# Targets read from SBUF, their PSUM bank given to layer 3 and the scores, in a DIN attention kernel on one core

## The reference

```
tgt = concat([target, pos]) @ proj_w + proj_b
din = concat([tgt, seq, tgt - seq, tgt * seq])
h = sigmoid(din @ w1 + b1)
h = sigmoid(h @ w2 + b2)
score = (h @ w3 + b3)[..., 0]
score = where(mask == 0, -1e9, score)
out = einsum('bs,bsd->bd', softmax(score), seq)
```

## Time and profile before

| What | Value |
|---|---|
| Median of 3 runs | 293.26 us |
| Profiled execution, time | 293.81 us |
| Its span | 292.0 us |
| Granted TensorE clock, mean over the span | 0.972 of full |
| TensorE busy | 250.3 us (86%) |
| VectorE busy | 235.7 us (81%) |
| GpSimd busy | 193.7 us (66%), all but 2 us of it after 66.3 us |
| ScalarE busy | 154.7 us (53%) |
| DMA queue of SyncE | 82.3% of 16 engines' span |

### The profile page before, as it was taken

How to read it: one execution, slowest core, us unless ns; L and a number is a source line. 1 busy time by engine, 2 the same in 40 slices (tenths; PEclk the granted TensorE clock), 3 DMA queues, 4 the chain that set the end, 5 groups by cost and what they waited for, 6 DMA issues and landing times.

```text
span 292.0 us, 5476 instructions
## 1 busy us (share of the span) xinstructions
PE 250.3 (86%) x2084; PEld 77.9 (27%) x2084; DVE 235.7 (81%) x331; ACT 154.7 (53%) x257; POOL 193.7 (66%) x125
## 2 busy tenths in 40 slices
PE   4659999999999999999999999999999999998100
PEld 2213323222322232323223323322233223222000
DVE  3598999689687886896887868968968799549696
ACT  2003467665666476556755674666566647656100
POOL 2000000009979979979799799797997997987970
PEclk9999999999999999999999999999999999999855
DMA  6989999999799999999999999899898860431200
GB/s 117 167 125 175 162 176 261 214 165 309 126 202 284 179 329 145 161 326 162 270 214 176 323 171 272 201 154 319 130 178 304 133 270 0 136 153 29 114 0 18
DMA packets 216749, 53.68 MB, mean 184 GB/s; under 512 B 209556, under 2 KB 210068, under 8 KB 216724
## 3 DMA queue, kind: packets, MB, share of 16 engines
q1 hardware_dynamic: 211640, 52.70, 82.3%
q10 hardware_dynamic: 5084, 0.64, 1.4%
HBM read 53.20 MB, written 0.13 MB: 183 GB/s over the span
## 4 chain that ended last, share of the span: by engine, by line
DVE 47%; PE 33%; issue 11%; POOL 3%; SPq 2%; DMA 1%; ACT 1%; DVEq 0%; ACTq 0%; POOLq 0%
DVE X L550 15%; PE pA L389 12%; DVE X L541 11%; DVE HidA L676 10%; PE pB L399 8%; PE pA L435 7%; DVE mix_v L637 3%; DVE HidB L683 2%; PE pA L445 2%; PE pL L415 2%; POOL mix L519 2%; POOL mix L508 1%; DVE pB L644 1%; PE pL L422 1%; DMA proj_b<-in_L_rec_proj_b 1%
## 5 line engine op out<-in xcount | busy, mean ns | idle before, releaser
L519 POOL TENSOR_TENSOR mix<-mix 128x260 f32<-128x260 f32 (+5 forms) x51 | 96.9, 1900 | 5.2 <-POOL acc L512 0.5
L277 ACT ACTIVATE HidA<-HidA,VA 128x512 f32<-128x512 f32 x100 | 66.8, 719 | 52.7 <-DVE HidA L676 52.7
L286 ACT ACTIVATE G<-pL,bias 128x512 f32<-128x512 f32 x100 | 60.5, 688 | 47.0 <-PE pL L422 47.0
L508 POOL TENSOR_TENSOR mix<-seq_sb,E 128x4096 f32<-128x4096 f32 (+3 forms) x13 | 77.2, 5941 | 0.4 <-POOL acc L523 0.3
L550 DVE SCALAR_TENSOR_TENSOR X<-pT,P_pair,X 128x512 f32<-128x512 f32 x100 | 69.8, 739 | 0.2
L676 DVE TENSOR_TENSOR HidA<-pA,UA 128x1024 f32<-128x1024 f32 x50 | 59.8, 1196 | 4.6 <-PE pA L389 4.2
L541 DVE STREAM_TRANSPOSE X<-squares 128x1024 f32<-128x1024 f32 x50 | 61.7, 1235 | 0.0
L389 PE MATMUL pA<-X,w_seq 64*64 64x512 f32 x400 | 55.0, 621 | 4.3 <-DVE HidA L676 3.7
L506 POOL MEMSET masked<- 128x64 f32 x11 | 1.7, 152 | 82.5 <-ACT E L319 82.5
L389 PE MATMUL pA<-X,w_sb 64*64 64x512 f32 x400 | 53.7, 608 | 0.0
L399 PE MATMUL pB<-X,wB 128*32 128x512 f32 x400 | 47.8, 596 | 0.0
(11 more groups left out here) (96 smaller groups left out, 106.1 us busy)
## 6 DMA issues: line engine op xcount, KB each, us to landing
squares<-in_L_rec_sequence_emb SPq DMA_DIRECT2D x98, 256.0 KB, 4.7
seq_sb<-in_L_rec_sequence_emb SPq DMA_DIRECT2D x12, 2048.0 KB, 9.9
seq_sb<-in_L_rec_sequence_emb SPq DMA_DIRECT2D x1, 1024.0 KB, 5.1
squares<-in_L_rec_sequence_emb ACTq DMA_DIRECT2D x2, 256.0 KB, 6.1
mask_i<-in_r_mask SPq DMA_DIRECT2D x1, 400.0 KB, 5.5
tgt_sb<-in_L_rec_target_emb SPq DMA_DIRECT2D x1, 128.0 KB, 2.2
out_dram<-result SPq DMA_DIRECT2D x1, 128.0 KB, 2.0
w_sb<-in_L_rec_w ACTq DMA_DIRECT2D x1, 80.0 KB, 3.8
```

Of the source, the lines that this page charges most:

```text
L277: last = nc.scalar.activation(h, h, ACT.Tanh, scale=0.5, bias=VA[:, 4 * u + i:4 * u + i + 1])
L286: nc.scalar.activation(G[p % NG][:, :], pL2[p % 4][:, :], ACT.Tanh, scale=0.5, bias=bias2[:, 0:1])\
L508: nc.gpsimd.tensor_tensor(mix[:, 0:k, 0:n, 0:D], seq_sb[c % RING][:, 0:k, 0:n, :], e[:, 0:k, 1:n + 1].unsqueeze(3).to_broadcast([P, k, n, ...
L519: nc.gpsimd.tensor_tensor(mix[:, 0:k, 0:n, :], mix[:, 0:k, 0:n, :], mix[:, 0:k, n:2 * n, :], ALU.add)\
```

## The change

`products` reads the targets from `T2` in SBUF in place of `pT` in PSUM, so all three operands of L550 are in SBUF. The bank `pT` is free for layer 3's scores and, after ScalarE has copied these out, for the transposed scores and the softmax step (`bank3`, `bank_st`); the last block uses two banks of `pL2`. `pA` is left to layer 1, so the waits on `s_za` in `layer3` and `transpose_scores` go, and so do two waits ahead of `layer1_first`. The copy to `rows` is made one iteration later, in the iteration of the transposes, ahead of layer 2's four Tanh. The transposes of the scores go ahead of `layer2_last`. On VectorE the second `transpose_quad` of an iteration goes ahead of the first pair's product, and the second pair's product goes behind the second `targets_first`. `shared_bank` becomes the two halves of `pA` and `pB`.

```
-    L2_LAG, L3_LAG, ST_LAG = 1, 2, 3
+    L2_LAG, L3_LAG, ROWS_LAG, ST_LAG = 1, 2, 3, 3
...
-        pL3, pST = pA[:, 0:512], pA[:, 512:1024]
+        def bank3(c):
+            return pT if c < NBLK - 1 else pL2[0]
+
+        def bank_st(c):
+            return pT if c < NBLK - 1 else pL2[1]
...
-        shared_bank = {SHARED: pT, SHARED + 1: pB, SHARED + 2: pL2[0]}
+        shared_bank = {SHARED: pA[:, 0:512], SHARED + 1: pA[:, 512:1024], SHARED + 2: pB[:, :]}
...
-                if 0 <= g < NGRP:
-                    for j in range(4):
-                        second_layer(4 * g + j)
-                c = block_of_last_group(n - L3_LAG)
+                c = block_of_last_group(n - ROWS_LAG)
                 if c is not None:
                     act.wait_ge(s_l3, c + 1)
                     if c > 0:
                         act.wait_ge(s_st, c)
+                    nc.scalar.activation(rows[:, :].rearrange("p (r k) -> p r k", k=SQ),
+                                         bank3(c)[:, :].rearrange("p (k r) -> p r k", r=TILE), ACT.Identity,
+                                         bias=bias3[:, 0:1]).then_inc(s_rows, 1)
+                if 0 <= g < NGRP:
+                    for j in range(4):
+                        second_layer(4 * g + j)
...
-            def layer3(c, quads):
-                pe.wait_ge(s_za, quads)
-                if c > 0:
-                    pe.wait_ge(s_rows, c)
+            def layer3(c):
+                if 0 < c < NBLK - 1:
+                    pe.wait_ge(s_soft, SOFT * c)
...
-            def transpose_scores(c, quads):
-                pe.wait_ge(s_za, quads)
-                if c > 0:
-                    pe.wait_ge(s_soft, SOFT * c)
+            def transpose_scores(c):
                 pe.wait_ge(s_rows, c + 1)
...
-                    c = block_of_last_group(n - 1 - L3_LAG)
-                    if c is not None:
-                        pe.wait_ge(s_rows, c + 1)
-                    c = block_of_last_group(n - 1 - ST_LAG)
-                    if c is not None:
-                        pe.wait_ge(s_soft, SOFT * (c + 1))
...
+                c = block_of_last_group(n - ST_LAG)
+                if c is not None:
+                    transpose_scores(c)
                 if 0 <= g < NGRP:
                     layer2_last(g)
-                c = block_of_last_group(n - ST_LAG)
-                if c is not None:
-                    transpose_scores(c, min(2 * n + 2, NQ))
...
+            def product(p):
+                dve.wait_ge(s_x1, p // 2 + 1)
+                if p >= NX:
+                    dve.wait_ge(s_l1b, (p - NX) // 4 + 1)
+                nc.vector.scalar_tensor_tensor(out=X2[p % NX][:, :], in0=T2[:, :], scalar=P_pair[:, p:p + 1],
+                                               in1=X1[p // 4 % 2][:, p % 4, :], op0=ALU.add, op1=ALU.mult)\
+                  .then_inc(s_x2, 1)
...
                 if n + 1 < NGRP:
-                    products(2 * n + 2)
                     transpose_quad(2 * n + 3)
+                    product(4 * n + 4)
                 if n < NGRP:
                     targets_first(2 * n + 1)
...
+                if n + 1 < NGRP:
+                    product(4 * n + 5)
                 c = block_of_last_group(n - ST_LAG)
                 if c is not None:
                     softmax_step(c)
                 if n + 1 < NGRP:
                     products(2 * n + 3)
```

More of the change, by code:

```diff
@@ L304, in _ @@
                         act.wait_ge(s_st, c)
-                    nc.scalar.activation(rows[:, :].rearrange("p (r k) -> p r k", k=SQ), pL3.rearrange("p (k r) -> p r k", r=TILE), ACT.Identity, bias=bias3[:, 0:1]).then_inc(s_rows, 1)
+                    nc.scalar.activation(rows[:, :].rearrange("p (r k) -> p r k", k=SQ),
[4 more added lines that the diff above has]
+                        second_layer(4 * g + j)
                 if n < NGRP:
@@ L313, in _ @@
                     if k < Q:
-                        if c == SHARED + 1:
+                        act.wait_ge(s_za, NQ)
+                        if c == SHARED + 2:
                             act.wait_ge(s_zb, NGRP)
@@ L434, in layer3 @@
                         p = c * BLK // 2 + j * per + k
-                        last = nc.tensor.matmul(pL3[j * TILE:(j + 1) * TILE, :], w3s[:, k, :], G[p % NG][:, :],
+                        last = nc.tensor.matmul(bank3(c)[j * TILE:(j + 1) * TILE, :], w3s[:, k, :], G[p % NG][:, :],
                                                 start=(k == 0), stop=(k == per - 1))
                 last.then_inc(s_l3, 1)
-            def transpose_scores(c, quads):
-                pe.wait_ge(s_za, quads)
-                if c > 0:
-                    pe.wait_ge(s_soft, SOFT * c)
+            def transpose_scores(c):
                 pe.wait_ge(s_rows, c + 1)
                 for q in range(Q):
-                    last = nc.tensor.transpose(pST[:, q * P:(q + 1) * P], rows[:, q * P:(q + 1) * P], ident[:, :])
+                    last = nc.tensor.transpose(bank_st(c)[:, q * P:(q + 1) * P], rows[:, q * P:(q + 1) * P], ident[:, :])
                 last.then_inc(s_st, 1)
@@ L468, in _ @@
                     setup_layer2()
+                c = block_of_last_group(n - ST_LAG)
+                if c is not None:
+                    transpose_scores(c)
                 if 0 <= g < NGRP:
                     layer2_last(g)
-                c = block_of_last_group(n - ST_LAG)
-                if c is not None:
-                    transpose_scores(c, min(2 * n + 2, NQ))
                 c = block_of_last_group(n - L3_LAG)
                 if c is not None:
-                    layer3(c, min(2 * n + 2, NQ))
+                    layer3(c)
                 if n < NGRP:
@@ L543, in transpose_quad @@
                   .then_inc(s_x1, 1)
+            def product(p):
[5 more added lines that the diff above has]
+                  .then_inc(s_x2, 1)
             def products(u):
-                dve.wait_ge(s_x1, u + 1)
                 for p in (2 * u, 2 * u + 1):
[L548 to L552, removed]
+                    product(p)
             dve.wait_ge(s_pset, TGT_TR)
@@ L646, in share_sum @@
                 nc.vector.tensor_tensor(acc[:, q0:Q, :], acc[:, q0:Q, :], part, ALU.add).then_inc(s_part, 1)
-            new_max = pST.rearrange("p (q x) -> p q x", q=Q)[:, :, TILE - 1:TILE]
             def softmax_step(c):
@@ L653, in softmax_step @@
                 x = n // NT
-                scores = pST.rearrange("p (q j x) -> p q j x", q=Q, j=NT)[:, :, :, 0:x]
+                scores = bank_st(c)[:, :].rearrange("p (q j x) -> p q j x", q=Q, j=NT)[:, :, :, 0:x]
+                new_max = bank_st(c)[:, :].rearrange("p (q x) -> p q x", q=Q)[:, :, TILE - 1:TILE]
                 dve.wait_ge(s_st, c + 1)
```

## The result

The changed kernel takes 383.01 us in the median of four runs (382.75 to 383.68); the kernel before, measured beside it, 294.5. The ratio is 1.301, 95% interval 1.292 to 1.309: slower, as forecast, and inside the range. The times of the kernel before lie in two groups, near 293.3 and 295.8 us, so its median moves between 293.3 and 294.5 from one occasion to the next.

What follows compares the result with a forecast made beforehand. TensorE's path was taken to set the pace. Exclusion adds 9.7 us to each of ten blocks, 97 us on the profiled 293.8, which with the median 0.5 us lower leaves 391 us; range 300 to 414 us.

Steps and rivals of the forecast that it cites:

- Part 3, the exclusion: Products with two SBUF tensors and GpSimd instructions reading SBUF exclude each other throughout: 9.7 us a block, chance 0.64.
- two bounds: Wait of each product beside GpSimd: from 0 us up to the running instruction's whole 7.07 us; the upper was taken.
- the waits, 12.5 a block: VectorE's products waiting for GpSimd in one block: 4.5, 4.5, 2.4 and 1.1 us.
- the point that I had at 21.9: End of the last two products' turns with GpSimd's sums, in us after the softmax step.
- the hand schedule: One block worked out from the end of the softmax step: 29.5 us in place of 19.8.
- The order at a release: Who goes first when both wait: VectorE's product always, 355 us; GpSimd's instruction always, 414 us.
- part 1: The freed bank removes TensorE's two waits, 1.0 us a block; moved transposes delay the exponentials by 0.6 us.
- Parts 1 and 2: Freed bank and VectorE's new order, without interplay: 0.6 us a block kept of 1.0, 6.5 us in all.
- VectorE's overrun, 0.4: VectorE's iteration with the softmax takes 9.4 us against TensorE's 9.0, holding TensorE up 0.4 us in the next iteration.
- The rival without interplay: Products and GpSimd don't slow each other and the two waits go: 287 us, chance 0.18.
- The fixed part of an SBUF operand: Product's fixed cost, 58 cycles from SBUF against 120 from PSUM by the skill: 0.065 us cheaper; rows show no gain.
- The rival of sharing: A product doubles while both stream, 0.74 us more: 3.2 us more a block, 326 us, chance 0.14.

Runs made afterwards that it cites:

- one edit: The kernel before, with only its products changed to read the targets from T2 in SBUF: 368.54 us, 1.250 of before.
- the pair with small GpSimd work: The kernel before and the changed kernel, each with GpSimd summing only the first feature of each history: 293.35 us (0.996) and 286.23 us (0.973).

## Why the prediction was right

**Part 3, the exclusion: right, as a mechanism.** The chosen end of the two bounds held: a product waits for the rest of the GpSimd instruction that is running (one edit reproduces it, cutting the instructions shrinks it, taking the length away removes it, and GpSimd's writing doesn't do it). The sentence of the Trainium skill (SBUF — State Buffer, Who interferes with whom) is borne out by these runs, down to its limit to GpSimd instructions that read. The argument from rows alone had been thin: "rates that don't stir there say nothing for a path that isn't used" was true, but it gave no reason for the upper bound, and without the sentence of the Trainium skill the choice of it would have been little better than a guess.

**Its size: 97 us forecast, 89.4 measured between the spans.** From the first softmax step to the eleventh it is 285.2 us (63.30 to 348.48) where it was 197.6 (63.52 to 261.11): 87.6 in place of 97, ten blocks of 28.5 on average where I had 29.5. The mis-sized terms are the waits, 12.5 a block and 11.8 by the rows above (4.65, 4.14, 2.13, 0.85 where I had 4.5, 4.5, 2.4, 1.1), and with them the price of a turn. I let each product begin its 0.70 us at GpSimd's end, and GpSimd's next instruction after it; but the product ends 0.55 after GpSimd's end, and the next sum is only 0.3 us longer and starts 0.08 after the one before. So a turn costs 0.4 us in place of 0.70, and the point that I had at 21.9 comes at 20.9 (286.47 less 265.55, the end of the softmax step). That is the 1.0 us a block. In one of the ten blocks the second product also came just ahead of GpSimd's first sum, the close call of the hand schedule, and went through in 0.73 us:

```profile
189.85 0.73 DVE L547 SCALAR_TENSOR_TENSOR X<-T,P_pair,X 128x512 f32<-128x512 f32 x1
```

```profile
189.96 5.08 POOL L517 TENSOR_TENSOR mix<-mix 128x2080 f32<-128x2080 f32 x1 [0.50 <-POOL acc L510]
```

There the sum is the one that waits, 5.08 us where its mean was 4.64, and the product behind it waits in its turn, so only 0.7 us of waits are saved.

The block was 29.6 us long all the same, since TensorE rested for longer there and came back at half its clock (VectorE waited 2.11 us for it ahead of L676, 0.37 in other blocks); the block behind it took 29.4, the other full ones 28.5 or 28.6, and the last, at the end of layer 1's work, 26.7. The cost of the slow restart was missing from my sum. The order at a release was the one taken: whoever waits goes next. Neither of the two ends (355 and 414 us) came about.

**Behind the last full block: 2.0 us not foreseen.** From the eleventh softmax step to the end it is 32.9 us in place of 30.9, and 32.1 against 29.7 in the pair with small GpSimd work: so it belongs to the moved instructions and not to the exclusion; the kernel with the one edit has 30.9 too. VectorE's order alone has 31.8 (257.99 to 289.8). Most of the 2.0 is the delay of the exponentials that part 1 put at 0.6 us and covered with GpSimd's idle time. In a block it is 0.9: the multiplication starts 3.8 us after the softmax step (264.80 to 268.62) where it was 2.9 (162.38 to 165.28). At the end it is 1.5: L506 starts 4.6 us after the step (348.48 to 353.05), where L508 started 3.1 after it (261.11 to 264.24), and there is no next block to cover it. 87.6 + 2.0, less 0.2 at the start, is 89.4.

**Parts 1 and 2: 1.0 us on offer right, what is kept too low.** Kept, without the exclusion, are 0.85 us a block, where I had 0.6. The estimate of VectorE's overrun, 0.4, was too high: 0.15 is missing from the 1.0, and 0.1 of it shows in the iteration behind the softmax, where L397 follows L423 after 1.82 us (179.92 to 181.74), just behind the end of VectorE's L676, and after 1.72 in the other iteration (190.02 to 191.74). The rival without interplay had 6.5 us of gain; the pair of small kernels gives 7.1. Under the exclusion VectorE sets the pace of the block; that nothing of the gain is left then, as written, was not measured by itself.

**The fixed part of an SBUF operand.** By the rows a product was to cost the same alone. By the Trainium skill (VectorE: DVE Perf Modes, the section on the TRN2 errata) it was to cost 0.065 us less, an estimate from its figures. Medians of 744 ns with both tensors in SBUF and 741 with one in PSUM decide for the rows.

**The rival of sharing, 326 us.** Nothing speaks for it any more: the loss follows the length of GpSimd's instructions, and a product of 5.54 us is more than the doubling that it allowed.

## What to carry to other kernels

Before an operand is moved from PSUM to SBUF, count the SBUF tensors of the VectorE instruction and look at what GpSimd reads at that time: here a second tensor made each such instruction wait out the reading GpSimd instruction that ran, so the price was that one's length and not the bytes. If it can't be avoided, shorter GpSimd instructions help, as the run with them cut in four shows; that fewer meetings help as well is argued, not tried. Look for a bank in time before you look in another memory: `pB` held nothing between L683 (164.44 us) and layer 1's next last matmuls, behind the L435 of 171.02, and the layout that uses this gap is the one that gained most.

## What the runs showed of the hardware

- With both tensors of a product in SBUF and GpSimd reading, the wait for GpSimd lies inside the duration of VectorE's instruction and counts as busy; no idle time and no releaser point to it. A spread from 0.70 to 5.54 us in instructions of one form was its mark here.
- It goes both ways and by turns: GpSimd's sums of 1.14 us became 1.41 on average, its copies of 0.30 us 0.77.
- Beside GpSimd's memsets of 3.5 us the same products keep 0.74 us.
- After 5.7 to 7.1 us of rest TensorE worked at half speed, at a granted clock of 0.50 from 201 to 206 us and from 282 to 285, 1.98 us for matmuls that take 1.09 at 2.4 GHz. In the block of 29.6 us a stall on another engine was so paid for twice.
